# First attention of a fused decoder: input and heads' result transposed by DMA instead of TensorE, projection of the output moved

## The chip, the cores and the metric

The kernel runs on one core of one Trainium2 chip. The metric is the device time of one execution in microseconds; of the kernel before, three runs gave a median of 1896.82 (1893.7 to 1897.35). The engines that matter are TensorE (PE; PEld is its weight load), VectorE (DVE), ScalarE (ACT), GpSimd (POOL) and SyncE (SP), whose queue issues DMAs.

## The reference

Two decoder layers on x of shape (16, 256, 256), in one kernel: layer norm and a decaying linear attention, layer norm and a causal cross attention, layer norm and a mixture of experts, then a time and channel mix, an attention with a bias, and a projection in float8. The change touches the second of these, here cut to what matters:

```python
def _L0_xattn_ref(q, k, v, mask, Wq, bq, Wk, bk, Wv, bv, Wo, bo):
    # q: the layer norm of x; k and v: the context; 16 heads of 16
    query = _dense_bf16(q, Wq, bq).astype(jnp.float32)
    key_p = _dense_bf16(k, Wk, bk).astype(jnp.float32)
    val_p = _dense_bf16(v, Wv, bv).astype(jnp.float32)
    ...
    x = _attention(query, key_p, val_p, mask)   # causal, and mask > 0
    x = x.transpose(0, 2, 1, 3).reshape(Bb, Lt, D_MODEL)
    out = _dense_bf16(x, Wo, bo)
    return out.astype(jnp.float32)

x = x + _L0_xattn_ref(_layernorm(x, axis=-1), ctx_1024, ctx_1024, mask_BxS2_if1, ...)
```

## The kernel before

x stays in SBUF (tile X) for the whole kernel. The stage `causal_attention` (prefix xa in the profile) takes one of the 16 batches a turn; a batch is 256 rows, two tiles of 128 (TB = 2), and 256 columns, two blocks of 128 (DC = 2). Each engine runs its own list of instructions, written out by hand; semaphores are all that orders them against each other. After the 16 turns come two that only drain.

A turn b has four steps g = 0 to 3 of four units, a unit being two heads on one tile of 128 queries. Steps 0 and 1 are the first tile, which by causality sees 128 keys, steps 2 and 3 the second, with 256. For each step TensorE makes scores (L846) in the banks p_s; VectorE subtracts the mask and takes the minimum (L1079, tiles sc and nmax); ScalarE takes the exponential (L999, pr); a step later TensorE transposes the result (L858, p_p), VectorE (L1088) and ScalarE (L984) copy every other unit to prT; and two steps later TensorE multiplies with v (L877, p_o), whose last column gives the sums. ScalarE reads the sums of half a batch (L990), TensorE turns them (L886), and VectorE divides (`normalise`, L1096 and L1100), which gives tile o of the batch before.

Between these lie the projections of the batch ahead and the output of one behind. All share one bank of PSUM, p_a, in a fixed order, each freed by the read of the one before:

- VectorE measures X of batch b+1 (L74, L77) in step 0, GpSimd takes the root (L83, L85), VectorE normalises to xn (L91) in step 1.
- Step 1: keys (PE L808, ACT L960, DVE L1053).
- Step 2: TensorE transposes xn, four blocks (L801), ScalarE reads them to xT (L948), TensorE projects the queries (L808), ScalarE reads q_r (L966), VectorE adds the bias and splits (L1063, L1066), all for b+1.
- Step 3: values (PE L816, ACT L972, POOL L766 and L768).
- Step 0: TensorE transposes o of batch b-2 (L801), ScalarE reads it to oT (L954), TensorE projects (L816), ScalarE reads y_r (L978), VectorE adds the bias (L1110), GpSimd adds to X (L773).

xn, xT, o, oT and the bank p_a are single; context, mask, q, k and v are double. The waits on the turned x (`turned_x`) and the turned o (`turned_o`) also free xn and o: `norm` and the first `normalise` of a turn wait for them. SP loads context and mask (L724, L725) for batch b+1 once GpSimd has used those of b-1, whose cast (L748), offsets (L753) and mask (L756) stand before the root in GpSimd's list.

Of the kernel before, what the change touches and what calls it, by code (L numbers as in the profile page):

```python
# [6 lines left out]
BF16 = mybir.dt.bfloat16  # L7
# [644 lines left out]
def causal_attention(nc, ins, X, sh, begun):  # L652
# [5 lines left out]
    with Phase(nc, "xa") as ph:  # L658
# [16 lines left out]
        p_ad = p_a[:, :].bitcast(BF16)[:, 0:512]  # L675
# [4 lines left out]
        names = ("measured var_eps rstd_ready normed turned_x "  # L680
                 "c_ready x_ready k_proj q_proj v_proj k_read q_read v_read k_ready q_ready v_ready off_ready neg_ready scored shifted exped p_turned p_copied_a p_copied_v "
                 "pv sums_read sums_turned o_ready turned_o oT_ready y_ready y_read y_biased added chain_v chain_p stood_v stood_p").split()
        s_ = {n: ph.sem(n) for n in names}
        ctx_in = [ph.sem(f"ctx_in{s}") for s in range(2)]
        raw_in = [ph.sem(f"raw_in{s}") for s in range(2)]
        block = ph.block()
# [34 lines left out]
        def _(sp):  # L721
# [5 lines left out]
            sp.dma_start(sh.a[:, 0:E * D + E * (HC + DC)], ins["pack_moe"]).then_inc(sh.sems["moe_in"], 16)  # L727
            for b, h, s in turns(sp):
                if has_next(b):
                    if b >= 2:  # L730
                        sp.wait_ge(s_["c_ready"], b - 1)
                        sp.wait_ge(s_["neg_ready"], b - 1)
                    load(b + 1, h + s, 1 - s)

        @block.gpsimd
        def _(pool):
# [38 lines left out]
            for b, h, s in long_turns(pool, drain=2):  # L775
                if has_next(b):
                    prepare(b + 1, h + s, 1 - s)
                    root(b + 1)
# [17 lines left out]
        def _(pe):  # L796
            def turn(tiles, done):

                for c in range(DC):
                    for t in range(TB):  # L800
                        last = pe.transpose(p_ad[:, c * S + t * P:c * S + (t + 1) * P], tiles(t)[:, c * P:(c + 1) * P], ident_d[:, :])  # L801
                last.then_inc(done, 1)

# [20 lines left out]
            def turn_x(n):  # L824
                pe.wait_ge(s_["normed"], n)
                pe.wait_ge(s_["k_read"], n)
                turn(lambda t: xn[:, t, :], s_["turned_x"])

            def project_queries(n):
                pe.wait_ge(s_["x_ready"], n)  # L830
                project(0, xT, s_["q_proj"])
# [57 lines left out]
            for b, h, s in long_turns(pe, drain=2):  # L889
                for g in range(STEPS if not at(b, B + 1) else 1):  # L890
                    if runs(b):
                        scores(b, s, g)
                    if g == 0 and since(b, 2):
                        if runs(b):
                            pe.wait_ge(s_["v_read"], b)
                        pe.wait_ge(s_["o_ready"], TB * (b - 1))
                        turn(lambda t: o[:, t, :], s_["turned_o"])
# [2217 lines left out]
```

## Time and profile before

| | |
|---|---|
| device time, three runs | 1896.82 us median, 1893.7 to 1897.35 |
| the profiled execution | 1893.5 us, its span 1891.7 us |
| PE busy | 1683.7 us, 89% |
| PEld busy | 1382.6 us, 73% |
| DVE busy | 1187.3 us, 63% |
| ACT busy | 1117.7 us, 59% |
| POOL busy | 683.4 us, 36% |

Busy shares are over the whole span, six stages with different limits; the first attention lies at about 84 to 402 us. Here a row of a timeline gives the start in us from the span's start, the time in us from the first start to the last end of what it merges, engine, line, operation, out<-in with shapes, and the count; in square brackets stands the idle time of the engine ahead of it and what ended it. Neighbouring instructions of one engine overlap a little, so the distance of two starts is often less than the duration.

### The profile page before, as it was taken

The page shows a single profiled execution, that of the slowest core. Times are in us where ns is not written, and L with a number is a line of the kernel's source. Part 1 is how long each engine was busy: PE and PEld are TensorE (multiplying, and loading weights), DVE is VectorE, ACT ScalarE, POOL GpSimd, SP SyncE. Part 2 cuts the span into 40 slices and gives each one's busy share as a digit, 9 for nine tenths or more (in the row PEclk, how much of TensorE's full clock was granted, in tenths as well). Part 3 has the DMA queues.
Part 4 walks back from the last instruction along what each step waited for, and adds up shares of the span by engine and source line. Part 5 has one row for each costly group of instructions (what it writes and reads, how often), then busy time and mean ns, then how long its engine had stood idle before and what let it go on. Part 6 is the DMA issues. An engine that isn't in the chain of part 4 may idle for free. (4 is left out here: it accounts for less than half of the span.)

```text
span 1891.7 us, 40735 instructions
## 1 busy us (share of the span) xinstructions
PE 1683.7 (89%) x13412; PEld 1382.6 (73%) x13412; DVE 1187.3 (63%) x4106; ACT 1117.7 (59%) x2571; POOL 683.4 (36%) x857
## 2 busy tenths in 40 slices
PE   6777777769999999999997899989999899999995
PEld 5555555557788888888996777777778677777774
DVE  6799999857301101011113899999985798888885
ACT  5599999942222222222334665666664788888894
POOL 4423232321211111110104466656654244445544
PEclk9899999979999999999998999999999899999998
DMA  3100010025855655655985200000000201111110
GB/s 131 49 19 27 19 27 19 3 79 187 274 174 176 201 178 169 202 178 161 332 270 168 73 23 20 15 23 23 23 29 1 74 23 34 35 36 35 36 63 29
DMA packets 111696, 171.96 MB, mean 91 GB/s; under 512 B 6832, under 2 KB 86576, under 8 KB 110864
## 3 DMA queue, kind: packets, MB, share of 16 engines
q1 hardware_dynamic: 95248, 142.55, 23.1%
q0 software_dynamic: 6480, 17.70, 3.2%
q10 hardware_dynamic: 9776, 9.31, 1.4%
q8 instruction: 101, 1.65, 0.4%
q14 instruction: 91, 0.75, 0.1%
HBM read 143.45 MB, written 26.08 MB: 90 GB/s over the span
## 5 line engine op out<-in xcount | busy, mean ns | idle before, releaser
L2151 ACT ACTIVATE moe_hT<-moe_p_h,lane_a 128x256 f32<-128x256 f32 (+1 forms) x344 | 131.4, 433 | 370.7 <-PE moe_p_h L2093 370.7
L2093 PE MATMUL moe_p_h<-moe_gT,moe_w 128*128 128x256 f32 (+1 forms) x1376 | 256.4, 345 | 0.8 <-issue 0.8
L2103 PE MATMUL moe_p_y<-moe_w,moe_hT 128*128 128x256 f32 x1136 | 252.3, 379 | 0.0
L2093 PEld LDWEIGHTS moe_p_h<-moe_gT,moe_w 128*128 128x128 f32 x1376 | 227.8, 192 | 25.8 <-issue 1.2
L1584 ACT ACTIVATE xb_pr<-xb_sc,xb_nmax 128x256 f32<-128x256 f32 x512 | 222.7, 503 | 29.9 <-DVE xb_nmax L1667 28.2
L1983 POOL DMA_INDIRECT moe_gx<-moe_tokens,moe_source_i x71 | 67.4, 949 | 457.5 <-PE moe_p_t L2080 401.5
L2103 PEld LDWEIGHTS moe_p_y<-moe_w,moe_hT 128*128 128x128 f32 x1136 | 212.5, 190 | 27.1
L999 ACT ACTIVATE xa_pr<-xa_sc,xa_nmax 128x256 f32<-128x256 f32 (+1 forms) x512 | 204.0, 452 | 21.3 <-DVE xa_nmax L1079 20.5
L1667 DVE CUSTOM_DVE_ANT_0 xb_sc<-xb_p_s,begun_area 128x256 f32<-128x256 f32 x512 | 187.1, 419 | 41.0 <-PE xb_p_s L1415 39.4
L2271 DVE COPY moe_gT<-moe_p_t 128x512 f32<-128x512 f32 (+1 forms) x43 | 25.7, 599 | 233.2 <-PE moe_p_t L2080 226.8
L2296 DVE TENSOR_TENSOR moe_gy<-moe_p_y,lane_a 128x256 f32<-128x256 f32 x71 | 27.6, 421 | 229.0 <-PE moe_p_y L2103 229.0
L1427 PE MATMUL xb_p_p<-ident,xb_pr 128*128 128x128 f32 x1024 | 145.5, 279 | 22.3 <-DVE xb_prT L1676 12.0
L1079 DVE CUSTOM_DVE_ANT_0 xa_sc<-xa_p_s,xa_neg 128x256 f32<-128x256 f32 (+1 forms) x512 | 151.7, 352 | 10.9 <-PE xa_p_s L846 9.2
L1427 PEld LDWEIGHTS xb_p_p<-ident,xb_pr 128*128 128x128 f32 x1024 | 112.3, 142 | 46.5 <-issue 27.2
L858 PE MATMUL xa_p_p<-ident,xa_pr 128*128 128x128 f32 x768 | 117.8, 281 | 21.4 <-DVE xa_prT L1088 15.7
L858 PEld LDWEIGHTS xa_p_p<-ident,xa_pr 128*128 128x128 f32 x768 | 83.5, 142 | 45.5 <-ACT xa_pr L999 24.5
L2609 PE MATMUL mix_p_kv<-mix_fv,mix_hid_sq 128*128 128x256 f32 x512 | 115.7, 379 | 0.0
L2703 PE MATMUL mix_p_h<-mix_mixed,mix_fk 128*128 128x256 f32 x512 | 114.2, 381 | 0.0
L2703 PEld LDWEIGHTS mix_p_h<-mix_mixed,mix_fk 128*128 128x128 f32 x512 | 98.3, 192 | 13.8
L2609 PEld LDWEIGHTS mix_p_kv<-mix_fv,mix_hid_sq 128*128 128x128 f32 x512 | 96.0, 190 | 12.8 <-ACT mix_hid_sq L2840 0.4
L1676 DVE COPY xb_prT<-xb_p_p 128x512 f32<-128x512 f32 x128 | 87.4, 683 | 6.4 <-PE xb_p_p L1427 6.4
L1557 ACT ACTIVATE xb_prT<-xb_p_p 128x512 f32<-128x512 f32 x128 | 75.1, 587 | 15.9 <-PE xb_p_p L1427 15.9
(376 smaller groups left out, 3442.1 us busy)
## 6 DMA issues: line engine op xcount, KB each, us to landing
moe_w<-in_L_ffn_w_dram SPq DMA_DIRECT2D x86, 1024.0 KB
begun_area<-xb_kv SPq DMA_DIRECT2D x32, 256.0 KB, 2.8
moe_rows_out<-moe_gy ACTq DMA_DIRECT2D x28, 256.0 KB
xb_kv<-moe_w SPq DMA_DIRECT2D x18, 256.0 KB, 4.9
X<-in_x_dram SPq DMA_DIRECT2D x4, 1024.0 KB, 9.5
xa_ctx<-in_ctx_turned_dram SPq DMA_DIRECT2D x16, 256.0 KB, 9.8
moe_tokens<-moe_XN_s SPq DMA_DIRECT2D x16, 256.0 KB, 2.3
xb_raw<-in_fside_BxSxS_dram SPq DMA_DIRECT2D x15, 256.0 KB, 3.7
```

The lines of the kernel that those rows point to most:

```text
L858: last = pe.transpose(p_p[m % 2][:, (e * TB + kt) * P:(e * TB + kt + 1) * P], pr[:, m % RB, e, kt * P:(kt + 1) * P], ident[:, :])
L999: last = act.activation(pr[:, n % RB, e, 0:width], sc[:, n % RB, e, 0:width], ACT.Exp, bias=nmax[:, n % RB, e:e + 1], scale=-1.0)
L1079: last = dve.tensor_tensor_reduce(out=sc[:, n % RB, e, 0:keys(t)], in0=scored_in(n, e), in1=neg[:, s, t, 0:keys(t)], scale=1.0, scalar=3e3 ...
L1427: last = pe.transpose(p_p[m % 2][:, (e * TB + kt) * P:(e * TB + kt + 1) * P], pr[:, m % RB, e, kt * P:(kt + 1) * P], ident[:, :])
L1584: last = act.activation(pr[:, n % RB, e, :], sc[:, n % RB, e, :], ACT.Exp, bias=nmax[:, n % RB, e:e + 1], scale=-1.0)
L1667: last = dve.tensor_tensor_reduce(out=sc[:, n % RB, e, :], in0=scored_in(n, e), in1=neg[:, s, t, :], scale=1.0, scalar=3e38, op0=ALU.add, ...
L1676: dve.tensor_copy(*turned_unit(m)).then_inc(s_["p_copied_v"], 1)
L2093: last = pe.matmul(p_h[n % 3][:, k * width:(k + 1) * width], w1[:, r, ic, (2 * n + k) * P:(2 * n + k + 1) * P], gT[:, r % 2, ic, 0:width], ...
L2103: last = pe.matmul(p_y[:, t * D:(t + 1) * D], hT[:, hc, t * P:(t + 1) * P], w2[:, r, hc, :], start=(hc == 0), stop=(hc == HC - 1))
L2151: last = act.activation(hT[:, 2 * n + k, 0:width], p_h[n % 3][:, k * width:(k + 1) * width], ACT.Gelu, bias=b1[:, bass.ds(e * HC + 2 * n + ...
L2609: last = pe.matmul(p_kv[:, t * D:(t + 1) * D], hid_sq[:, hc, t * P:(t + 1) * P], fv[:, hc, :], start=(hc == 0), stop=(hc == HC - 1))
L2703: last = pe.matmul(p_h[m % 2][:, k * S:(k + 1) * S], fk[:, ic, (2 * m + k) * P:(2 * m + k + 1) * P], mixed2[:, 0, ic, :], start=(ic == 0), ...
```

## The change

The four transposes of xn and the four of o leave TensorE, with ScalarE's reads of them. SP issues two DMA transposes for each instead, SBUF to SBUF, 128 rows by 256 columns of bfloat16 each, into the same tiles xT and oT. Measuring, root and normalising of x go a turn further ahead (batch b+2), so that in turn 0 batches 1 and 2 are both done. The projection of the output, its read and its bias move from step 0 to step 2. TensorE's q projection then waits for the read of the projected output, and SP's list has the transposes between the loads. The diff, cut to its core:

```diff
             sp.dma_start(sh.a[:, 0:E * D + E * (HC + DC)], ins["pack_moe"]).then_inc(sh.sems["moe_in"], 16)
+            def turn_x(n):
+                sp.wait_ge(s_["normed"], n)
+                if n >= 2:
+                    sp.wait_ge(s_["q_proj"], n - 1)
+                for t in range(TB):
+                    sp.dma_start(xT[:, :, t * P:(t + 1) * P], xn[:, t, :], transpose=True).then_inc(xT_in, 16)
+
+            def turn_outputs(n):
+                if n >= 1:
+                    sp.wait_ge(s_["y_ready"], n)
+                for t in range(TB):
+                    sp.wait_ge(s_["o_ready"], TB * n + t + 1)
+                    sp.dma_start(oT[:, :, t * P:(t + 1) * P], o[:, t, :], transpose=True).then_inc(oT_in, 16)
+
             for b, h, s in turns(sp):
                 if has_next(b):
                     if b >= 2:
                         sp.wait_ge(s_["c_ready"], b - 1)
                         sp.wait_ge(s_["neg_ready"], b - 1)
                     load(b + 1, h + s, 1 - s)
+                if b == 0:
+                    turn_x(1)
+                if has_next(b, 2):
+                    turn_x(b + 2)
+                if b >= 1:
+                    turn_outputs(b - 1)
+            turn_outputs(B - 1)
...
             for b, h, s in long_turns(pool, drain=2):
                 if has_next(b):
                     prepare(b + 1, h + s, 1 - s)
-                    root(b + 1)
+                if b == 0:
+                    root(1)
+                if has_next(b, 2):
+                    root(b + 2)
                 if since(b, 2):
...
             def project_queries(n):
-                pe.wait_ge(s_["x_ready"], n)
+                pe.wait_ge(xT_in, 16 * TB * n)
                 project(0, xT, s_["q_proj"])
+
+            def project_outputs(n):
+                pe.wait_ge(oT_in, 16 * TB * (n + 1))
+                project_rows(oT, 3, s_["y_ready"])
...
                 for g in range(STEPS if not at(b, B + 1) else 1):
                     if runs(b):
                         scores(b, s, g)
-                    if g == 0 and since(b, 2):
-                        if runs(b):
-                            pe.wait_ge(s_["v_read"], b)
-                        pe.wait_ge(s_["o_ready"], TB * (b - 1))
-                        turn(lambda t: o[:, t, :], s_["turned_o"])
-                    if g == 2 and has_next(b):
-                        turn_x(b + 1)
+                    if at(b, B + 1):
+                        pe.wait_ge(s_["o_ready"], TB * B)
+                        project_outputs(B - 1)
+                    if g == 2 and since(b, 2):
+                        if has_next(b):
+                            pe.wait_ge(s_["k_read"], b + 1)
+                        else:
+                            pe.wait_ge(s_["o_ready"], TB * (b - 1) + 1)
+                        project_outputs(b - 2)
                     if g == 3 and since(b, 1):
                         if has_next(b):
                             pe.wait_ge(s_["q_read"], b + 1)
-                        else:
-                            pe.wait_ge(s_["o_ready"], TB * (b - 1) + 1)
+                        elif b >= 2:
+                            pe.wait_ge(s_["y_read"], b - 1)
                         turn_sums(TB * b)
                     m = unit_before(b, g, 1)
                     if m is not None:
                         turn_unit(b, m)
                         turn_unit(b, m + 1)
-                    if g == 0 and since(b, 2):
-                        pe.wait_ge(s_["oT_ready"], b - 1)
-                        project_rows(oT, 3, s_["y_ready"])
                     if g == 1 and has_next(b):
                         if since(b, 1):
                             pe.wait_ge(s_["o_ready"], TB * (b - 1) + 1)
                         project_keys(b + 1)
                     if g == 2 and has_next(b):
+                        if b >= 2:
+                            pe.wait_ge(s_["y_read"], b - 1)
+                        else:
+                            pe.wait_ge(s_["k_read"], b + 1)
                         project_queries(b + 1)
...
-            def read_x(n):
-                act.wait_ge(s_["turned_x"], n)
-                if n >= 2:
-                    act.wait_ge(s_["q_proj"], n - 1)
-                act.activation(flat(xT[:, :, :]), p_ad, ACT.Copy).then_inc(s_["x_ready"], 1)
-
-            def read_outputs(n):
-                act.wait_ge(s_["turned_o"], n + 1)
-                if since(n, 1):
-                    act.wait_ge(s_["y_ready"], n)
-                act.activation(flat(oT[:, :, :]), p_ad, ACT.Copy).then_inc(s_["oT_ready"], 1)
...
-                    if g == 0 and since(b, 2):
-                        read_outputs(b - 2)
-                    if g == 2 and has_next(b):
-                        read_x(b + 1)
                     m = unit_before(b, g, 1)
                     if runs(b):
                         exponentials(b, STEP * g)
+                    if g == 2 and since(b, 2):
+                        read_projected(b - 2)
                     if m is not None:
                         copy_unit(b, m + 1)
                     if runs(b):
                         exponentials(b, STEP * g + 1)
-                    if g == 0 and since(b, 2):
-                        read_projected(b - 2)
+                    if at(b, B + 1):
+                        read_projected(B - 1)
                     if g == 1 and has_next(b):
...
                 dve.wait_ge(s_["rstd_ready"], n)
                 if n >= 2:
-                    dve.wait_ge(s_["turned_x"], n - 1)
+                    dve.wait_ge(xT_in, 16 * TB * (n - 1))
                 layer_norm_apply(dve, lambda t: tile_of(X, n, t), lambda t: xn[:, t, :], aggr, rstd, s_["normed"])
...
                 if t == 0 and since(b, 1):
-                    dve.wait_ge(s_["turned_o"], b)
+                    dve.wait_ge(oT_in, 16 * TB * b)
...
-                    if g == 0 and has_next(b):
-                        measure(b + 1)
-                    if g == 0 and since(b, 2):
-                        bias_output(b - 2)
-                    if g == 1 and has_next(b):
-                        norm(b + 1)
+                    if g == 0:
+                        if at(b, 0):
+                            measure(1)
+                        elif has_next(b, 2):
+                            measure(b + 2)
+                    if g == 2 and at(b, 0):
+                        measure(2)
+                    if at(b, B + 1):
+                        bias_output(B - 1)
+                    if g == 1 and b >= 1 and has_next(b, 2):
+                        norm(b + 2)
+                    if g == 1 and at(b, 0):
+                        norm(1)
+                    if g == 3 and at(b, 0):
+                        norm(2)
                     if m is not None:
                         copy_unit(b, m + 2)
                     if g == 1 and has_next(b):
                         finish_keys(b + 1, 1 - s)
+                    if g == 2 and since(b, 2):
+                        bias_output(b - 2)
                     if g == 2 and has_next(b):
                         finish_queries(b + 1, 1 - s)
                 chain.close()

```

## Rows read from the trace of the kernel before

**Rows 1.** Windows, a steady turn: us, PE, PEld, DVE, ACT, POOL busy, PEclk, DMA, GB/s.
```profile
223.29:242.46 19.17, 15.09 (x209) 10.40 (x208) 17.73 (x93) 18.22 (x48) 6.34 (x11) 1.00 0.09 24
```

**Rows 2.** Timeline of ScalarE in that turn: start, us, what, count, [idle before].
```profile
223.82 0.69 ACT L999 ACTIVATE xa_pr<-xa_sc,xa_nmax 128x128 f32<-128x128 f32 x2 [0.93 <-DVE xa_nmax L1079]
227.66 0.59 ACT L948 ACTIVATE xa_xT<-xa_p_a 128x512 bf16<-128x512 bf16 x1
228.13 0.91 ACT L999 ACTIVATE xa_pr<-xa_sc,xa_nmax 128x256 f32<-128x256 f32 x2
229.99 0.59 ACT L966 ACTIVATE xa_q_r<-xa_p_a 128x512 bf16<-128x512 f32 x1
233.29 0.57 ACT L984 ACTIVATE xa_prT<-xa_p_p 128x512 f32<-128x512 f32 x1
237.71 0.58 ACT L954 ACTIVATE xa_oT<-xa_p_a 128x512 bf16<-128x512 bf16 x1
238.77 0.59 ACT L984 ACTIVATE xa_prT<-xa_p_p 128x512 f32<-128x512 f32 x1
```

**Rows 3.** Timeline of VectorE in the same turn.
```profile
227.63 0.08 DVE L1079 DVE_READ_ACCUMULATOR2_ANT xa_nmax<- 128x1 f32 x1
230.03 0.42 DVE L1088 COPY xa_prT<-xa_p_p 128x256 f32<-128x256 f32 x1
230.62 0.48 DVE L1063 TENSOR_SCALAR xa_q_f<-xa_q_r,xa_cols_d 128x256 bf16<-128x256 bf16 x2 [0.17 <-ACT xa_q_r L966]
231.67 0.42 DVE L1079 CUSTOM_DVE_ANT_0 xa_sc<-xa_p_s,xa_neg 128x256 f32<-128x256 f32 x1
239.01 0.74 DVE L74 BATCH_NORM_STATS2 xa_stats<-X 128x6 f32<-128x256 f32 x2
240.45 0.49 DVE L1110 TENSOR_TENSOR xa_y_f<-xa_y_r,xa_rows_d 128x256 bf16<-128x256 bf16 x2 [0.41 <-ACT xa_y_r L978]
241.76 0.26 DVE L1096 RECIPROCAL xa_inv<-xa_p_a 128x16 f32<-128x16 f32 x1 [0.21 <-PE xa_p_a L886]
```

**Rows 4.** Timeline of TensorE there: transposes of x, q projection, transposes after it.
```profile
226.61 0.40 PE L801 MATMUL xa_p_a<-xa_ident_d,xa_xn 128*128 128x128 bf16 x4
228.30 0.61 PE L808 MATMUL xa_p_a<-xa_xT,lane_b 128*128 128x256 bf16 x4 [0.85 <-ACT xa_xT L948]
228.88 0.41 PE L858 MATMUL xa_p_p<-ident,xa_pr 128*128 128x128 f32 x2
```

**Rows 5.** Timeline of SP's queue: the slowest issue, and a load in that turn.
```profile
125.50 1.83 SPq L725 DMA_DIRECT2D xa_raw<-in_mask_BxS_if_dram  x1
240.17 0.38 SPq L724 DMA_DIRECT2D xa_ctx<-in_ctx_turned_dram  x1
```

**Rows 6.** DMA issues by tile: count, KB each, median us from issue to landing.
```profile
begun_area<-xb_kv SPq DMA_DIRECT2D x32, 256.0 KB, 2.8
xb_kv<-mix_hid SPq DMA_DIRECT2D x14, 256.0 KB, 2.1
```

**Rows 7.** Timeline of GpSimd before the root, and VectorE's normalising after it.
```profile
237.34 0.61 POOL L748 CAST xa_cT<-xa_ctx 128x512 bf16<-128x512 f32 x1
240.61 0.71 POOL L85 TENSOR_TENSOR xa_rstd<-xa_rstd,minus_half 128x2 f32<-128x2 f32 x1 [0.18 <-POOL xa_rstd L83]
244.48 0.73 DVE L91 TENSOR_SCALAR xa_xn<-X,xa_aggr,xa_rstd 128x256 bf16<-128x256 f32 x2
```

**Rows 8.** Timeline of turns 0 and 1: normalising, q projection, first division.
```profile
92.16 0.73 DVE L91 TENSOR_SCALAR xa_xn<-X,xa_aggr,xa_rstd 128x256 bf16<-128x256 f32 x2 [5.14 <-POOL xa_rstd L85]
94.25 1.06 PE L808 MATMUL xa_p_a<-xa_xT,lane_b 128*128 128x256 bf16 x4
107.49 0.26 DVE L1096 RECIPROCAL xa_inv<-xa_p_a 128x16 f32<-128x16 f32 x1 [1.25 <-PE xa_p_a L886]
```

**Rows 9.** Timeline of the last turn: last o, and its projection.
```profile
396.83 0.49 DVE L1100 TENSOR_TENSOR xa_o<-xa_p_a,xa_inv 128x128 bf16<-128x128 f32 x2
398.46 0.61 PE L816 MATMUL xa_p_a<-lane_b,xa_oT 128*128 128x256 bf16 x4 [0.69 <-ACT xa_oT L954]
```

More of the change, by code:

```diff
@@ L674, in causal_attention @@
         p_a = ph.ps("p_a")
-        p_ad = p_a[:, :].bitcast(BF16)[:, 0:512]
         p_s = [ph.ps(f"p_s{i}") for i in range(4)]
@@ L678, in causal_attention @@
         p_o = ph.ps("p_o")
-        names = ("measured var_eps rstd_ready normed turned_x "
-                 "c_ready x_ready k_proj q_proj v_proj k_read q_read v_read k_ready q_ready v_ready off_ready neg_ready scored shifted exped p_turned p_copied_a p_copied_v "
-                 "pv sums_read sums_turned o_ready turned_o oT_ready y_ready y_read y_biased added chain_v chain_p stood_v stood_p").split()
+        names = ("measured var_eps rstd_ready normed "
+                 "c_ready k_proj q_proj v_proj k_read q_read v_read k_ready q_ready v_ready off_ready neg_ready scored shifted exped p_turned p_copied_a p_copied_v "
+                 "pv sums_read sums_turned o_ready y_ready y_read y_biased added chain_v chain_p stood_v stood_p").split()
         s_ = {n: ph.sem(n) for n in names}
@@ L685, in causal_attention @@
         raw_in = [ph.sem(f"raw_in{s}") for s in range(2)]
+        xT_in = ph.sem("xT_in")
+        oT_in = ph.sem("oT_in")
         block = ph.block()
@@ L796, in _ @@
         def _(pe):
[L797 to L802, printed above, removed]
             def project(n, src, done):
@@ L822, in project_keys @@
                 project(1, cT, s_["k_proj"])
[L824 to L827, printed above, removed]
             def project_queries(n):
-                pe.wait_ge(s_["x_ready"], n)
+                pe.wait_ge(xT_in, 16 * TB * n)
                 project(0, xT, s_["q_proj"])
+            def project_outputs(n):
+                pe.wait_ge(oT_in, 16 * TB * (n + 1))
+                project_rows(oT, 3, s_["y_ready"])
             def project_values(n):
@@ L930, in _ @@
                     if g == 0 and since(b, 1) and not at(b, B + 1):
-                        if since(b, 2):
-                            pe.wait_ge(s_["y_read"], b - 1)
+                        if runs(b):
+                            pe.wait_ge(s_["v_read"], b)
                         else:
-                            pe.wait_ge(s_["v_read"], b)
+                            pe.wait_ge(s_["o_ready"], TB * (b - 1))
                         turn_sums(TB * (b - 1) + 1)
```

## The prediction, made before the changed kernel was run

> **What bounds the kernel now.** The change lies in the first attention alone, so I read one steady turn (one batch) of it first: 19.17 us [rows 1], and the sixteen of them are about a sixth of the 1891.7 us span. ScalarE is busy 18.22 us of that turn, VectorE 17.73, TensorE 15.09, at a granted clock of 1.00, the 2.4 GHz level: two engines close to full, so shares don't say what a removed instruction is worth. I therefore took one turn (223.3 to 242.5) engine by engine and followed it back from its one large hole, ScalarE's 0.93 us wait at 223.82 [rows 2]. It waits for VectorE, which had just done the division of step 1; the division waits 0.21 us for TensorE's turned sums (at 241.76) [rows 3], TensorE came to these through the transposes of the unit that ScalarE copied at 238.77 to 239.36, and from there ScalarE ran without a gap back to about 232.5. There it is VectorE again: the first mask-and-minimum unit of step 3 starts at 231.67 and, 0.77 us after its start like the unit that ends at 227.71 [rows 3], is done at 232.44. ScalarE's exponential of it starts 0.80 us before the copy at 233.29 [rows 2], at 232.49. And VectorE is late there because its query step waits 0.17 us for ScalarE's read of q (229.99, 0.59 us). So the loop that sets the turn is: ScalarE up to the q read at 230.58, VectorE 230.62 to 232.44, ScalarE 232.49 to 239.36, TensorE and VectorE back to 242.5. Two reads go away; one lies in each ScalarE part.
>
> **The change part by part, in a steady turn.**
> *Read of the turned o* (ScalarE, step 0): gone. From its start to the next instruction's is 0.47 us (the other read, 227.66 to 228.13, shows the same [rows 2]); its 0.58 us duration overlaps the next. It lies in the second ScalarE part: -0.47 us.
> *Read of the turned x* (step 2): gone, -0.47; but the read of the projected output moves from step 0 into step 2, before the q read: +0.47. Net nothing on this part. The exponential ahead of it can start at 227.74 (its minimum is there at 227.71), so the moved read runs 228.54 to 229.13. Out of step 0 it saves nothing: after 239.36 the loop is on TensorE, and it stood later in ScalarE's list.
> *q projection*: the new wait for that read (it frees the shared bank) takes the place of the wait for the turned x. It started at 228.30 [rows 4]; now 229.20, +0.90. Behind it in TensorE's order are the transposes that VectorE's second copy of the step needs: the first now ends at 229.20+0.58+0.41+0.06 = 230.25, where the copy stood at 230.03 [rows 3]: +0.22. (0.58 is from its start to the transposes' start at 228.88, 0.41 theirs, 0.06 for a semaphore.)
> *Bias of the output* (VectorE): leaves step 0, where it costs 0.42 and waits 0.41, and where VectorE then only waits longer at 241.76 (it stands ready some 0.5 us early); it enters step 2 between that copy and the query step. Copy at 230.25, +0.34, bias +0.42: the query step starts at 231.01 instead of 230.62, +0.39, and swallows its 0.17 wait. Step 3 starts 0.39 later, and ScalarE's exponential too.
> *TensorE*: eight transposes less, 0.40 us for four [rows 4], and no waits of 0.7 to 0.9 us for the two reads; it was not the limit in these places. Cover: its idle time. The output projection, 0.58 us, moves to step 2, where the read of k, a step earlier, has freed the bank.
> Sum of the turn: +0.39 - 0.47 = -0.08 us, a turn of 19.1 us. The gain is on ScalarE, the toll on VectorE, and the loop passes through both. If the copy does not wait (+0.22 gone) it is -0.30. The output reads sit in turns 2 to 15, so 14 turns: **-1.1 us** (bound -4.2).
>
> *DMA transposes*: four a turn, 64 KB each, on SP's queue. No row shows one. How long one holds the queue (T): from below 0.38 us, a plain issue, from above by the slowest issue of this stage, 1.83 us [rows 5]. I take 0.5, since most issues are at the lower end. Landing after issue: rows of 256 KB show 2.1 (to DRAM) and 2.8 us (from it) [rows 6]; I take 2.4. In the steady turn this is hidden: x is issued after the former q projection ends, 229.9, and needed one turn later (18 us of cover); o's second half is issued after 233.8, and the next division, which now waits for it, stands at 241.76: 8 us of cover against 2.9.
> *SP's order*: the load of context and mask stood two turns ahead, at 240.17 [rows 5]; now it is behind the transposes, whose last waits for the division of step 3 (233.82, +0.39). Issue near 234.8, landing by 237.6 to 238; GpSimd turned to it at 237.3, ends its chain with the root at 241.32, and VectorE wants the root at 244.48 [rows 7]. 3 us of cover, at least 2 of them left.
> *POOL, measuring and normalising two turns ahead*: same instructions, a turn earlier. GpSimd's add waits for a bias half a turn later; the queue behind it (values' bias) is wanted only when v is read in step 3.
>
> **Start.** Turn 0 now measures and normalises twice. The normalised x is there at 92.89; q projection started at 94.25 [rows 8]. Now two issues and a landing: 92.9+0.1+0.4+2.4 = 95.8, +1.6 us. VectorE meanwhile has the extra measuring (1.0 us, the stretch of 239.01 to 240.0 [rows 3]) and the extra normalising (0.65); it passes the query step 1.0 late, and the later 0.65 goes into its 1.25 us wait of turn 1 [rows 8]. Since 95.8 plus the 1.06 of the projection there is before VectorE's need at 97.6, the larger counts: **+1.0 us** (0 if the waits hide all, 2.5 if landing takes 4).
> **End.** The last o is ready at 397.32 and its projection started at 398.46 [rows 9], 1.14 us. A DMA needs 0.1+2.4 = 2.5: +1.4. Turn 16 saves one read of 0.47: **+0.9 us** (0.4 to 2).
> **Sum.** -1.1+1.0+0.9 = +0.8 us. The profiled execution took 1893.5 us (span 1891.7, 1.8 around it), and so would become 1894.3; it stands 3.3 below the median 1896.82, to which I add the same: 1897.6.
>
> **A rule against this.** The rows show four 128x128 bf16 transposes on TensorE in 0.40 us [rows 4], with one read of 0.59 us behind [rows 2]. The Trainium skill (VectorE: DVE Perf Modes, "The three transpose paths") gives the crossbar 1309 ns for such a block against 390 on TensorE, and advises TensorE where PSUM will do. At two blocks a DMA that estimate is T = 2.6 us; no run here shows it yet, and it is what the rival "queue" would need. It also gives (DMA: Bandwidth & Descriptors, "Anatomy of one DMA") about 2.0 us fixed per DMA; the 2.1 and 2.8 us landings agree.
>
> **Rivals.**
> *Queue* (slower). The place is SP's queue: q projection ends (229.9 in the changed turn), four transposes of T, then the load, 2.8 us landing, 4.0 us of GpSimd (237.34 to 241.32), VectorE's normalising at 244.48, a little later (244.8) in the new order. 229.9+4T+2.8+4.0+0.1 = 244.8 gives the point where it decides: T = 2.0 us. Above it each turn grows by 4(T-2.0). At T = 2.6: 2.4 x 14 = 34 us, 1932. For it: nothing in the trace prices T, and its upper bound of 1.83 is close. Against: a plain issue is at 0.38, and 64 KB is a quarter of the context load. Chance 0.14.
> *Moved work binds more* (slower). The wait for the moved read, or the bias, costs VectorE 0.3 us a turn more than I worked out, as when the second transpose too is late for ScalarE's copy: 14 x 0.3 = 4.2, with +0.8: 1902. For it: VectorE and TensorE already trade waits in step 2 (0.85 us at 228.30). Chance 0.14.
> *VectorE absorbs* (faster). The +0.39 vanishes in its slack and the o read counts in full: 14 x 0.47 = 6.6 less 1.9: 1892.1. Chance 0.12.
> *Both reads count* (faster), the turn being ScalarE's 95% share: 14 x 0.94 = 13.2 less 1.9: 1885.5. Against: the share argument ignores the read that only moves. Chance 0.08.
> *As worked out*, 1897.6, 1893 to 1900: 0.52.
>
> **How the numbers follow.** The likeliest is 1897.6. The range, 1890 to 1912, takes in the two small cases on either side and the small overshoots of T (T = 2.2 gives +12), and leaves out the full ScalarE gain and most of the queue case: about 2 in 10. Within 0.2% (3.8 us, about what can be told from no change here): 0.53. Faster: 0.12+0.08 = 0.20. Slower: 0.14+0.14 less what lies below the bound: 0.27.
>
> **What would show it.** Right: a turn of 19.0 to 19.2 us; ScalarE busy 17.3 of it with a longer wait before step 1's first exponential (1.3 to 1.5 us); q's step on VectorE without a wait, right behind the bias; TensorE's q projection waiting for the moved read; landings near 2.5 us; no wait of VectorE for oT, none of GpSimd for context beyond 0.7 us. Wrong: GpSimd waiting for context several us each turn (queue); VectorE's division waiting for a DMA; a turn under 18.8 (one of the faster cases).

## The result, and the profile after

The changed kernel takes 1917.85 us in the median of six runs (1915.07 to 1921.64), the kernel before on the same chip 1895.82 (six runs); the ratio is 1.0118, 95% interval 1.0103 to 1.0132. It is 22 us slower. I had forecast 1897.6, from 1890 to 1912: the time lies outside the range.

The profiled execution took 1915.37 us, its span 1913.6. Counted from SP's load of the MoE's weights that opens the stage, over ScalarE's reads of q (one a turn, 15 in all), to the load that follows the stage, the two traces stand like this:

| | before | after | difference |
|---|---|---|---|
| start of the stage to the read of q in turn 1 | 33.03 us | 38.15 | +5.1 |
| the 13 turns from there | 249.35 (19.18 each) | 265.74 (20.44 each) | +16.4 |
| from the last read of q to the end of the stage | 38.50 | 41.73 | +3.2 |
| the rest of the kernel | 1570.8 | 1568.0 | -2.8 |

So the turns carry it. They are of two kinds. Windows of three turns of the changed kernel, cut at the read of q (columns as in [rows 1]):

```profile
223.67:244.54 20.87, 15.37 (x208) 11.07 (x200) 18.35 (x93) 17.59 (x48) 6.50 (x10) 0.92 0.15 35
268.32:289.13 20.81, 15.25 (x200) 11.28 (x200) 18.55 (x95) 17.65 (x48) 6.50 (x10) 0.92 0.14 36
289.13:308.78 19.65, 14.16 (x200) 10.13 (x200) 18.34 (x93) 17.27 (x47) 6.50 (x10) 1.00 0.14 35
```

Against the 19.17 us of [rows 1], ScalarE is busy 0.6 to 1.0 us less, as meant, and VectorE 0.6 to 0.8 us more, though it was given nothing new. Of the 12 turns from the third on, nine look like the first two rows (a mean granted clock of 0.92) and three like the last (1.00).

Where VectorE's extra time lies: its timeline in step 2 of the turn that ends at 244, with GpSimd's add of the output to X beside it (it answers [rows 3]).

```profile
243.62 0.43 DVE L1094 COPY xa_prT<-xa_p_p 128x256 f32<-128x256 f32 x1
243.96 0.48 DVE L1116 TENSOR_TENSOR xa_y_f<-xa_y_r,xa_rows_d 128x256 bf16<-128x256 bf16 x2
244.36 0.47 DVE L1069 TENSOR_SCALAR xa_q_f<-xa_q_r,xa_cols_d 128x256 bf16<-128x256 bf16 x2
244.62 1.24 POOL L795 TENSOR_TENSOR X<-xa_y_f,X 128x512 f32<-128x512 bf16 x1 [7.45 <-DVE xa_y_f L1116]
244.87 1.41 DVE L1072 TENSOR_SCALAR xa_q<-xa_q_f,parity 128x512 bf16<-128x512 bf16 x2
```

The bias is done at 244.44, GpSimd's add starts on it at 244.62, and the two instructions that split q (the last of the query step, L1072) take 1.41 us. They end at 246.28, 0.42 after the add's end at 245.86. In the kernel before the same two took 0.62, and the add lay in step 0, where VectorE's division ran beside it at its usual 0.26 and 0.49 us. It is one of the two that stands, not both (first line: shortest, median and longest of the changed kernel's 30, in ns; then rows of the kernel before):

```profile
L1072 DVE TENSOR_SCALAR xa_q<-xa_q_f,parity x30: 341/350/1147, 100.1 to 389.5; 128x512 bf16<-128x512 bf16 x30
231.14 0.62 DVE L1066 TENSOR_SCALAR xa_q<-xa_q_f,parity 128x512 bf16<-128x512 bf16 x2
241.30 1.17 POOL L773 TENSOR_TENSOR X<-xa_y_f,X 128x512 f32<-128x512 bf16 x1
242.06 0.49 DVE L1100 TENSOR_TENSOR xa_o<-xa_p_a,xa_inv 128x128 bf16<-128x128 f32 x2
```

The bill is larger than 0.79 us, since step 3 hangs on it. TensorE there, of two turns with the clock falling and one without:

```profile
248.41 0.94 PE L834 MATMUL xa_p_a<-lane_b,xa_cT 128*128 128x256 bf16 x4 [2.24 <-DVE xa_o L1106]
249.15 1.91 PE L875 MATMUL xa_p_p<-ident,xa_pr 128*128 128x128 f32 x8
269.23 1.04 PE L834 MATMUL xa_p_a<-lane_b,xa_cT 128*128 128x256 bf16 x4 [2.25 <-DVE xa_o L1106]
270.05 1.92 PE L875 MATMUL xa_p_p<-ident,xa_pr 128*128 128x128 f32 x8
289.92 0.61 PE L834 MATMUL xa_p_a<-lane_b,xa_cT 128*128 128x256 bf16 x4 [2.24 <-DVE xa_o L1106]
290.60 1.07 PE L875 MATMUL xa_p_p<-ident,xa_pr 128*128 128x128 f32 x8
```

TensorE's projection of values (L834) waits for the division of step 3, which VectorE reaches 0.79 us later; its idle time in front grows from 1.45 us (at 233.88 of the kernel before) to 2.24. Behind that idle time the granted clock is at its lower level, 1.2 GHz, in most turns: eight transposes take 1.91 us instead of 1.07. A window over the second of these stretches shows the clock itself, 0.50:

```profile
269.20:272.00 2.80, 2.77 (x16) 2.23 (x20) 2.63 (x10) 2.20 (x6) 0.83 (x2) 0.50 0.19 44
```

Such a turn is about 1.15 us longer than one at 2.4 GHz.

SP's queue, which I had feared, in one turn, and the landings (DMA issues, median us from issue to landing):

```profile
243.45 2.48 SPq L734 DMA_TRANSPOSE xa_xT<-xa_xn  x2
246.03 3.52 SPq L741 DMA_TRANSPOSE xa_oT<-xa_o  x2
249.65 0.53 SPq L725 DMA_DIRECT2D xa_ctx<-in_ctx_turned_dram  x1
xa_oT<-xa_o SPq DMA_TRANSPOSE x32, 2.3
xa_xT<-xa_xn SPq DMA_TRANSPOSE x30, 2.4
```

One transpose holds the queue for about 1.24 us (of the 3.52, about 1.1 is the wait for o's second half). In four of the last 12 turns one of x's two held it longer, so that the pair took 2.8 to 3.3 us; no run shows why. No engine's wait in the steady turns is put down to a transpose.

### The profile page after: what moved, and what is told of

The parts are those of the page before. It is cut to its first block and busy times, and to the rows that moved or that the text cites. A ratio compares the mean times of both kernels' runs of the same rounds, so it can differ in the third digit from the quotient of the medians.

```text
span 1913.6 us, 40515 instructions
## 1 busy us (share of the span) xinstructions
PE 1683.2 (88%) x13283; PEld 1390.9 (73%) x13288; DVE 1199.0 (63%) x4106; ACT 1106.5 (58%) x2540; POOL 687.2 (36%) x857
## 5 line engine op out<-in xcount | busy, mean ns | idle before, releaser
L875 PE MATMUL xa_p_p<-ident,xa_pr 128*128 128x128 f32 x768 | 122.0, 300 | 32.0 <-DVE xa_prT L1094 27.0
L875 PEld LDWEIGHTS xa_p_p<-ident,xa_pr 128*128 128x128 f32 x768 | 94.5, 154 | 50.7 <-ACT xa_pr L1007 31.0
L1574 ACT ACTIVATE xb_prT<-xb_p_p 128x512 f32<-128x512 f32 x128 | 75.0, 586 | 15.9 <-PE xb_p_p L1444 15.9
```

Of the source, the lines that this page charges most:

```text
L875: last = pe.transpose(p_p[m % 2][:, (e * TB + kt) * P:(e * TB + kt + 1) * P], pr[:, m % RB, e, kt * P:(kt + 1) * P], ident[:, :])
L1574: act.activation(*turned_unit(m), ACT.Copy).then_inc(s_["p_copied_a"], 1)
```

## The experiments

Theory A, from the trace: two instructions of VectorE that read SBUF stand still while GpSimd's add runs (0.79 us), and TensorE's longer idle time then costs the clock (up to 1.15 us more). Rivals: the new order of bias and query step by itself; the DMA queue with the load of context behind it; the start and the end. In all diffs below the base is the changed kernel unless another is named.

**no_add.** The add is left out, so X lacks the output of the first attention.

```diff
-                pool.tensor_tensor(X[:, bass.ds(TB * b, TB), :], y_f[:, :, :], X[:, bass.ds(TB * b, TB), :], ALU.add).then_inc(s_["added"], 1)
+                pool.sem_inc(s_["added"], 1)
```

> The changed kernel with GpSimd's add of the output to X left out (the semaphore is still raised; X keeps its value, so all later stages compute on other numbers). Theory A (collision): the add, 1.24 us, now starts with the bias done and runs beside VectorE's bfloat16 split of q, which takes 1.41 us for two instead of 0.62; the 0.79 us are on the path and widen TensorE's wait for the division in step 3 to 2.24 us, after which its granted clock falls to half in 10 of 13 turns. Without the add: the split back at 0.62, the wait at about 1.45, clock 1.00, turn 19.7 - 0.8 = 18.9 us in all turns, the kernel near 1893. Theory B (the moved projection alone slows the turn and the clock): the split is back at 0.62 but turns stay near 20, clock near 0.92. Theory C (DMA traffic slows VectorE's access to SBUF): the split stays at 1.4.

One run: 1891.7 us, against 1894.26 for the kernel before (14 runs, 1889.31 to 1901.56), so the whole time says little and the trace has to. From the third on the turns are 18.86 to 19.00 us, all at 2.4 GHz, and TensorE's idle time is back at its old length:

```profile
254.37 0.61 DVE L1072 TENSOR_SCALAR xa_q<-xa_q_f,parity 128x512 bf16<-128x512 bf16 x2
257.11 0.61 PE L834 MATMUL xa_p_a<-lane_b,xa_cT 128*128 128x256 bf16 x4 [1.45 <-DVE xa_o L1106]
```

One instruction of GpSimd, which is busy a third of the turn, is worth 1.5 us a turn (the mean of the 13 turns goes from 20.44 to 18.90). It does not yet say whether by its place or by its being there.

**fill.** TensorE is kept busier: in step 3 the transposes of the second unit are done three times. The added work is useless.

```diff
                         turn_unit(b, m)
-                        turn_unit(b, m + 1)
+                        turn_unit(b, m + 1, 3 if g == 3 and runs(b) else 1)
```

> The changed kernel, but in step 3 TensorE repeats the transposes of the second unit twice more (8 transposes, the same values), so that its idle time before the values' projection shrinks from 2.24 to about 1.2 us. It does only harm as work. Theory A (idle gap lets the clock fall): clock 1.00 in every turn, turns of 19.7 us instead of 20.8 in 10 of 13, that is 11 to 12 us less than the changed kernel: 1906. Rival (the clock falls for another reason, or a lower clock costs nothing): no change or slower, 1918 or more.

1907.09 us in the median (1901.75 to 1914.53); ratio 1.0076 (1.0052 to 1.0099). More work on TensorE makes the kernel some 10 us faster than the change as it stands; in the profiles 10.5 us of it lie in the 13 turns. Every turn from the third on is 19.65 to 19.82 us at a clock of 1.00, the length of the rare turns of the changed kernel, with the split of q as slow as ever:

```profile
256.59 1.41 DVE L1072 TENSOR_SCALAR xa_q<-xa_q_f,parity 128x512 bf16<-128x512 bf16 x2
260.12 0.61 PE L834 MATMUL xa_p_a<-lane_b,xa_cT 128*128 128x256 bf16 x4 [1.37 <-DVE xa_o L1106]
260.81 1.06 PE L875 MATMUL xa_p_p<-ident,xa_pr 128*128 128x128 f32 x8
```

This parts the two halves of theory A: the collision alone is 19.65 - 18.87 = 0.78 us a turn, the clock the rest. What kept the clock up, the added work or the shorter idle time (1.37 us), this run can't tell, since it has both.

**late_add.** The kernel before, with GpSimd's add moved against VectorE's query step and nothing else changed: no DMA transposes, no moved projection.

```diff
                 wait_alone(pool, s_["stood_p"], (s_["y_biased"], b + 1))
+                if has_next(b, 3):
+                    wait_alone(pool, s_["stood_p"], (s_["q_read"], b + 3))
```

> The kernel before, with one more wait: GpSimd's add to X waits for the read of q, so that it runs beside VectorE's q step as in the changed kernel. Nothing else differs. Theory A: the split of q (0.62 us for two) takes about 1.4, TensorE's wait before the values' projection grows from 1.45 to about 2.2, the clock falls in most turns, and each turn grows by 0.8 to 1.9 us: 12 x 0.8 to 12 x 1.9 = 10 to 23 us, 1906 to 1918. Rival B (the loss is due to DMA or the moved projection): 1896, the split at 0.62.

1912.13 us (1909.71 to 1917.68); ratio 1.0094 (1.0058 to 1.0129). Its turns are 20.1 us at the full clock and 20.8 where the clock falls (8 of the last 12), against 19.18. Here the add meets the bias of q, the instruction just ahead of the split, and that one is slow:

```profile
240.89 1.40 DVE L1065 TENSOR_SCALAR xa_q_f<-xa_q_r,xa_cols_d 128x256 bf16<-128x256 bf16 x2 [0.18 <-ACT xa_q_r L968]
241.03 1.17 POOL L775 TENSOR_TENSOR X<-xa_y_f,X 128x512 f32<-128x512 bf16 x1 [8.25 <-ACT xa_q_r L968]
242.32 0.62 DVE L1068 TENSOR_SCALAR xa_q<-xa_q_f,parity 128x512 bf16<-128x512 bf16 x2
245.06 0.61 PE L818 MATMUL xa_p_a<-lane_b,xa_cT 128*128 128x256 bf16 x4 [2.37 <-DVE xa_o L1102]
```

So the collision is enough to slow the kernel before by some 18 us, without any part of the change.

**bias_behind_q.** VectorE's bias of the output goes behind the query step, and the add with it.

```diff
-                    if g == 2 and since(b, 2):
-                        bias_output(b - 2)
                     if g == 2 and has_next(b):
                         finish_queries(b + 1, 1 - s)
+                    if g == 2 and since(b, 2):
+                        bias_output(b - 2)
```

> The changed kernel with VectorE's bias of the output behind the split of q instead of ahead of it. Theory A: the 0.42 us of the bias and the collision both leave the path to the first mask unit's start in part: the split at 0.62, its start 0.42 earlier, but the bias then follows before step 3, so step 3 is 0.8 earlier than in the changed kernel. The add runs beside the mask units, which read PSUM in float32; if these are not slowed, turns of 18.9 us, clock 1.00, near 1903 with the start and end losses still in. If they are slowed, no gain. Rival B: only the order of equal work, 1917.

1906.08 us; ratio 1.0064 (1.004 to 1.0087). The split is at 0.61 us again, yet six of the last 12 turns are 19.9 to 20.1 us at a clock of 0.91 to 0.92, the others 19.2 at 1.00, where I had expected 18.9 in all. The query step now stands ahead of the bias and waits 0.24 us for the read of q, and the bias still comes before step 3, so that the division is late:

```profile
278.54 0.48 DVE L1069 TENSOR_SCALAR xa_q_f<-xa_q_r,xa_cols_d 128x256 bf16<-128x256 bf16 x2 [0.24 <-ACT xa_q_r L974]
262.12 0.61 PE L834 MATMUL xa_p_a<-lane_b,xa_cT 128*128 128x256 bf16 x4 [1.78 <-DVE xa_o L1106]
262.81 1.61 PE L875 MATMUL xa_p_p<-ident,xa_pr 128*128 128x128 f32 x8
```

The order that avoids the collision costs 0.33 us of its own, and half the turns still lose the clock.

**add_behind_q.** The order of VectorE stays as the change has it; GpSimd's add alone waits until q is split.

```diff
                 wait_alone(pool, s_["stood_p"], (s_["y_biased"], b + 1))
+                if has_next(b, 3):
+                    wait_alone(pool, s_["stood_p"], (s_["q_ready"], b + 3))
```

> The changed kernel with one more wait in GpSimd's list: the add to X waits until the split of q is done, so it runs beside the mask units instead. Nothing is left out. Theory A: split at 0.62 for two, turns of 18.9 us at clock 1.00 as without the add, 13 turns give 20 us back: 1897 to 1899 (start and end losses stay, against 1894 to 1896 of before). Rival A2 (the add slows the mask units as well, as the half throttled turns of 19.2 to 20.0 with the bias behind q leave open): turns of 19.2 to 20, 1903.

1897.88 us (10 runs); ratio 1.0012 (0.9992 to 1.0032): one wait takes back 19 of the 22 us. A steady turn is 18.87, as without the add. In it VectorE runs step 2 without a gap, the add lies beside the mask units of step 3, and these keep their 0.41 to 0.42 us:

```profile
236.80 0.62 DVE L1074 TENSOR_SCALAR xa_q<-xa_q_f,parity 128x512 bf16<-128x512 bf16 x2
237.33 0.41 DVE L1087 CUSTOM_DVE_ANT_0 xa_sc<-xa_p_s,xa_neg 128x256 f32<-128x256 f32 x1
237.59 1.16 POOL L797 TENSOR_TENSOR X<-xa_y_f,X 128x512 f32<-128x512 bf16 x1 [7.08 <-DVE xa_q L1074]
238.02 0.42 DVE L1087 CUSTOM_DVE_ANT_0 xa_sc<-xa_p_s,xa_neg 128x256 f32<-128x256 f32 x1
```

So it is the add's place that costs, not its existence.

**load_first** and **add_q_load.** The load of context and mask goes back ahead of the transposes, two turns ahead: in the changed kernel, and in add_behind_q.

```diff
-                if has_next(b):
-                    if b >= 2:
-                        sp.wait_ge(s_["c_ready"], b - 1)
-                        sp.wait_ge(s_["neg_ready"], b - 1)
-                    load(b + 1, h + s, 1 - s)
+                if b == 0:
+                    load(1, h + s, 1 - s)
+                if has_next(b, 2):
+                    if b >= 1:
+                        sp.wait_ge(s_["c_ready"], b)
+                        sp.wait_ge(s_["neg_ready"], b)
+                    load(b + 2, h + 1, s)
```

> The changed kernel, but SP issues the load of batch b+2 ahead of the transposes in its list (after the context and mask of b are used) instead of the load of b+1 behind them. Theory D (part of the start loss is the load queued behind the transposes): in the changed kernel the load for turn 1 is issued at 108.5, GpSimd waits 6.3 us for it, TensorE 2.4, VectorE 3.6, and the second q read comes 38.15 us after the stage's start instead of 33.03. With the load first: 34.5 to 35, so 3 to 3.6 us less, no wait of GpSimd for context in any turn, steady turns unchanged near 19.7 and 20.8: 1914. Rival (the start loss is only the doubled measuring and the landing): 38, 1918.

> The changed kernel with both repairs: the add waits for the split of q, and the load goes ahead of the transposes. Theory A and D together: turns of 18.9 us, clock 1.00, second q read 34.5 to 35 us after the stage's start: 1893 to 1895, within 0.2% of before. If the two losses overlap rather than add: 1897.

1912.42 us, ratio 1.0083 (1.0055 to 1.0111), and 1895.4, ratio 0.9997 (0.9981 to 1.0014): 5.4 and 2.5 us less than their bases, but each interval overlaps that of its base, so the times alone don't settle it. In the profiles a steady turn at the full clock stays as it is (19.65 and 18.87). Up to the read of q in turn 1 it is 1.3 us less (36.81 against 38.15) and 0.9 (36.50 against 37.37), where I had expected more than 3 in load_first: GpSimd no longer waits for context in turn 1, but in both runs the first load of all is used some 2 us later. The rest is the clock, which no row ties to the load: it fell in seven of the last 12 turns of load_first instead of nine (2.6 us), and add_behind_q has one early turn of 20.11 us at 0.87 that takes 18.90 in add_q_load. What the place costs is plainest in the changed kernel: there the load for turn 1 stands behind x's second pair of transposes, which waits for a normalising at 104.85.

```profile
97.82 1.01 PE L826 MATMUL xa_p_a<-xa_xT,lane_b 128*128 128x256 bf16 x4 [2.33 <-DMA xa_xT<-xa_xn]
104.85 1.11 DVE L91 TENSOR_SCALAR xa_xn<-X,xa_aggr,xa_rstd 128x256 bf16<-128x256 f32 x2
108.50 0.58 SPq L725 DMA_DIRECT2D xa_ctx<-in_ctx_turned_dram  x1
113.45 0.61 POOL L770 CAST xa_cT<-xa_ctx 128x512 bf16<-128x512 f32 x1 [6.28 <-DMA xa_ctx<-in_ctx_turned_dram]
117.42 0.74 DVE L91 TENSOR_SCALAR xa_xn<-X,xa_aggr,xa_rstd 128x256 bf16<-128x256 f32 x2 [3.62 <-POOL xa_rstd L85]
```

So at the start the queue does hold up GpSimd and VectorE; in the steady turns no row shows it.

**step0_load** and **step0.** The projection of the output, its read and its bias return to step 0; the DMA transposes stay. With the early load, and without it. The core of the edit on VectorE, and the same on TensorE and ScalarE:

```diff
-                    if at(b, B + 1):
-                        bias_output(B - 1)
+                    if g == 0 and since(b, 2):
+                        bias_output(b - 2)
...
-                    if g == 2 and since(b, 2):
-                        bias_output(b - 2)
```

> The changed kernel with the projection of the output, its read and its bias back in step 0, and the load ahead of the transposes: only the transposes by DMA and the input two turns ahead remain of the change. Worked out from the rows: ScalarE saves 0.47 in its second part, and in the first VectorE's 0.17 wait before the q step; turn 19.17 - 0.64 = 18.5, or 18.9 if TensorE stands for the second half of o at the start of step 0 (issued 234.3, landing 2.4 later, wanted 236.4). No collision of the add with a bfloat16 step. Start +1.5, end +1.4. 14 x 0.64 = 9 less 3: 1889; with 18.9: 1894. Rival (moving the projection was needed: the wait for o holds up step 0 by over 1 us): over 1900.

> The changed kernel with the projection of the output, its read and its bias back in step 0, as in the run step0_load, but the load of context and mask left where the change puts it, behind the turn's transposes. It tells what the place of the load is worth by itself. If the load's place matters at the start alone (the load for turn 1 issued behind the transposes of batch 2, GpSimd waiting 6 us for context), the turns stay at 18.42 us, the start grows by 1 to 3 us against step0_load, and the kernel takes 1889 to 1891. If GpSimd's wait for context also costs the steady turns once they are this short, a turn is 18.6 or more and the kernel takes 1892 or more. If neither, 1887.6.

1887.6 us (12 runs, 1884.82 to 1890.2), ratio 0.9957 (0.994 to 0.9975), and 1888.5 (12 runs), ratio 0.9974 (0.9959 to 0.9988). Both are faster than the kernel before, by 7.4 and 6.1 us in the medians. A turn is 18.42 us:

```profile
228.39:246.81 18.42, 14.41 (x208) 10.14 (x209) 17.59 (x93) 17.34 (x47) 6.49 (x10) 1.00 0.15 38
```

The DMA transposes, with x measured and normalised a turn further ahead, thus save 0.76 us a turn, of the 0.94 that ScalarE's two reads were worth; moving the projection takes 0.45 of that back (18.87), the collision 0.78 and the clock up to 1.15 more. As to the load, the profile shows 3.2 us less at the start with it early (34.94 against 38.14), and the same turns but for three of 18.6 to 18.8; the medians differ by 0.9 us, and the intervals overlap, so the times do not settle that.

**transposes_twice.** On add_behind_q: each transpose is issued a second time into a tile that nobody reads, and the waits cover both.

```diff
                     sp.dma_start(oT[:, :, t * P:(t + 1) * P], o[:, t, :], transpose=True).then_inc(oT_in, 16)
+                    sp.dma_start(oT2[:, :, t * P:(t + 1) * P], o[:, t, :], transpose=True).then_inc(oT_in, 16)
```

> The changed kernel with GpSimd's add behind q_ready, as in the run add_behind_q, and each of SP's four transposes of a turn issued a second time, into tiles that nobody reads; every wait for a transpose waits for both. What the queue costs when it does bind. In add_behind_q the load of context is issued at 240.78, GpSimd waits 0.66 us for it at 243.72, its root ends at 247.95 and VectorE normalises at 249.66: 1.7 us of slack. Four more transposes at the 1.23 us that each holds the queue are 4.9 us; the last of them wait for o less than before, so the load comes some 4.5 us later. By the queue theory (the transposes hold SP's queue one after another, and the loop q projection, transposes, load, GpSimd, normalising binds once its slack is used up) a turn grows from 18.87 to between 20.7 (threshold as predicted, 4 x (2.46 - 2.0)) and 21.7 (4.5 - 1.7), GpSimd waits 4 to 5 us for context and VectorE for the root, and the kernel takes 1923 to 1938. By the rival theory (the second transposes hide, as they move only 64 KB each and nobody needs them) the time stays within 3 us of 1897.9 and GpSimd's wait for context stays near 0.7 us.

1960.08 us in the median of three runs (1959.8 to 1964.81); a fourth took 9350.69 us, and no trace shows why. The ratio is 1.0341 (1.0321 to 1.0361): the queue theory's sign, and more than its size. A turn is 23.2 us in the mean, 4.2 more than the 18.99 of add_behind_q, and a clock of 0.84 to 0.92. The queue, and who waits:

```profile
245.35 1.25 SPq L737 DMA_TRANSPOSE xa_xT<-xa_xn  x1
247.93 2.15 SPq L745 DMA_TRANSPOSE xa_oT<-xa_o  x1
232.67 0.61 POOL L774 CAST xa_cT<-xa_ctx 128x512 bf16<-128x512 f32 x1 [6.00 <-DMA xa_ctx<-in_ctx_turned_dram]
236.82 0.74 DVE L91 TENSOR_SCALAR xa_xn<-X,xa_aggr,xa_rstd 128x256 bf16<-128x256 f32 x2 [3.13 <-POOL xa_rstd L85]
252.75 0.53 SPq L727 DMA_DIRECT2D xa_ctx<-in_ctx_turned_dram  x1
```

From the end of the q projection (241.47) to the load it is now 11.3 us, against 5.5 (235.29 to 240.78) in add_behind_q: 5.8 more, where I had written 4.5. Four more transposes at 1.29 us from start to start are 5.2, in this turn one held the queue for 2.15 instead of 1.25, and add_behind_q had waited some 0.25 for o's second half, which is now there in time. Over the turns from the third on the path is 5.2 us longer in the mean (10.9 against 5.6). The slack that I had put at 1.7 us is that of one turn of add_behind_q; in its turns it goes from 0.24 to 1.77, with a mean of 1.0. 5.2 less 1.0 is 4.2, as measured; what part the lower clock has in it was not separated. The loop (q projection, transposes, load, GpSimd, normalising) therefore binds, in the mean, from a hold of about 1.25 + 1.0/4 = 1.5 us (an estimate from these rows), and add_behind_q at 1.24 stands 1 us a turn short of it, in some turns only 0.24. In the changed kernel, whose turns are longer, the slack is 0.77 to 2.5 us.

## Why the prediction was wrong

**The step that failed** is the one line on GpSimd: "GpSimd's add waits for a bias half a turn later; the queue behind it (values' bias) is wanted only when v is read in step 3." I asked who waits for GpSimd's queue, found nobody, and costed the moved add at nothing. I did not ask what VectorE does in the 1.2 us beside it. The price could have been read in the trace of before, though in another stage, near the kernel's end. There VectorE normalises two tiles from SBUF to SBUF beside a GpSimd operation of the same kind, and needs 1.57 us for what takes 0.73 [rows 7, 8], and it ends where GpSimd's operation ends plus one tile (rows of the kernel before):

```profile
1880.12 1.17 POOL L1338 TENSOR_TENSOR xb_f_y<-xb_f_y,lane_b 128x512 f32<-128x512 f16 x1
1880.19 1.57 DVE L91 TENSOR_SCALAR xb_f_xn<-X,xb_f_aggr,xb_f_rstd 128x256 f32<-128x256 f32 x2 [1.33 <-POOL xb_f_rstd L85]
```

In the first attention it cost 0.79 us a turn on the loop, 12 times: 9.5 us.

**The second failure** follows. Of TensorE I wrote "it was not the limit in these places. Cover: its idle time." Its idle time was the very thing that was not free. Nine turns at the lower clock cost 1.15 us each, 10.4 us. Together with the -4.0 us that the 13 turns gain (13 times 18.87 - 19.18) this gives 15.9 of the 16.4 us measured.

**The turn without the two** came out at the edge that I named: 18.87, which is -0.31, where I took -0.08 and gave -0.30 as the case in which VectorE's copy does not wait. It does not: in add_behind_q the copy of step 2 starts as the unit ahead of it ends. The q projection did move by 0.9 us against VectorE, as forecast: it starts 2.25 us behind VectorE's first mask unit of the step (234.68 against 232.43), before it was 1.36 (228.30 against 226.94). What was too long is the stretch behind it, "229.20+0.58+0.41+0.06 = 230.25": 1.05 us from the projection's start to the copy, which starts after 0.87 (235.55), as the transposes follow the projection after 0.45 us instead of 0.58. The rest of the sum holds: VectorE's step 2 is 0.17 us longer (4.90 instead of 4.73), ScalarE's read saves 0.47, which makes the -0.31. Other signs were as forecast: ScalarE 17.36 us busy with 1.41 us of wait before step 1's first exponential, the query step right behind the bias, landings at 2.3 and 2.4 us, and no wait for oT. One was not: GpSimd waits for context longer than the 0.7 us that I allowed, 0.27 to 1.91 us a turn in the changed kernel and 0.66 to 1.93 in add_behind_q; but VectorE's normalising does not wait in the steady turns.

**The queue.** T was 1.24 us, where I took 0.5 between 0.38 and 1.83. The rival needed 2.0 by my working and about 1.5 by the doubled run, so it did not decide in the steady turns, but it was nearer than I had it. The Trainium skill's 1309 ns a block (VectorE: DVE Perf Modes, "The three transpose paths") would have made 2.6 us of it, read as a hold of the queue; so read, the trace disagrees: 1.24 us for two blocks in the queue, with a landing of 2.3 to 2.4 from issue. The 2.0 us per DMA that the prediction took from the Trainium skill stand in a section on transfers that GpSimd issues, and these are SP's; no term of the sum went by them.

**The start** was the wrong size: +5.1 us instead of +1.0. The normalised x to the q projection took 3.9 us (93.92 to 97.82) instead of 2.9, because the second transpose is issued 1.3 us behind the first and not 0.4, and lands 2.4 later; and the step on SP's order looked at the steady turn only, where it found 3 us of cover. In turn 1 there is none: GpSimd waits 6.28 us. load_first gives 1.3 us of the start back and step0_load, against step0, 3.2 (its first load is not late); what remains at the start (1.9 us in step0_load) was not taken apart further.

**The end**: from the last o to its projection 2.46 us, where I wrote 2.5, but at the lower clock, and behind one collision more. The whole end is +3.2; without the collision (add_behind_q) it is +1.3, against +0.9 forecast:

```profile
421.34 0.49 DVE L1106 TENSOR_TENSOR xa_o<-xa_p_a,xa_inv 128x128 bf16<-128x128 f32 x2
424.29 1.01 PE L834 MATMUL xa_p_a<-lane_b,xa_oT 128*128 128x256 bf16 x4 [3.28 <-DMA xa_oT<-xa_o]
```

That add_behind_q, at 1897.88, meets the forecast of 1897.6 almost to the tenth is chance: a gain of 2.5 us in the turns instead of 1.1, and a start of +4.3 instead of +1.0.

**Both reads count**, the rival at 1885.5, was refused because "the share argument ignores the read that only moves". That was right for this change, and step0_load shows that it was the move that was wrong: leave the projection where it was, and the kernel takes 1887.6.

## What to carry to other kernels

When an instruction of GpSimd moves, look at which instructions of VectorE it then lies beside: a share of a third says nothing of the place, and one wait that holds GpSimd until VectorE's SBUF-to-SBUF stretch is over gave back 19 of 22 us here. When a stall of another engine makes TensorE's pause longer, price the clock as well as the pause. And when a change has two parts, here a transpose by DMA (good for 0.76 us a turn) and a moved projection (bad for at least 0.45), run them apart.

## What the runs showed of the hardware

- **VectorE beside GpSimd.** Instructions of VectorE that take a tensor of bfloat16 in SBUF with a scalar and write SBUF stand still beside a GpSimd tensor_tensor on SBUF: two of 128x512 went from 0.62 to 1.41 us, two of 128x256 from 0.48 to 1.40. A pair that had begun when the add started kept its 0.47 us (the bias of q at 244.36). Those that read PSUM (mask units 0.42, division 0.26 and 0.49) were not slowed by the same add. The Trainium skill (SBUF — State Buffer, "SBUF: two separate sides") says that the port pair the two engines share is an exclusive lock and not a split of bandwidth, for VectorE operations that use both ports; the rows agree, in that one instruction takes 1.15 us and the other its usual 0.35, and the pair ends 0.42 us after the add; that these instructions use both ports no row shows.
- **TensorE's clock.** With 1.36 to 1.45 us of idle time ahead of the values' projection (fill, no_add, add_behind_q), and with 1.58 (step0 and step0_load), the granted clock stayed at 2.4 GHz in all of the last 12 turns; with 1.78 us it fell to 1.2 GHz in 6 of 12 (bias_behind_q), with 2.24 in 9 of 12 (the changed kernel) and 7 of 12 (load_first), with 2.37 in 8 of 12 (late_add). The same idle time does not always end the same way. Useless transposes on TensorE, 16 instead of 8 in a row, kept it up and made the kernel faster.
- **DMA transposes from SBUF to SBUF**, 128x256 of bfloat16: 1.24 us of the issuing queue in most cases (now and then 1.5 to 2.7), 2.3 to 2.4 us from issue to landing, and one behind the other the next starts 0.04 us after. A plain load of 256 KB held the same queue for 0.4 to 0.6 us in the steady turns.
